# Last stage of a gated two-layer block: projections laid behind the scores in smaller pieces, and two gates ahead of the joining of keys

## The reference

```
x = x + tanh(g_xattn[0]) * L0_xattn(layernorm(x), ctx, ctx)      # causal, 16 heads of 32
x = x + tanh(g_ffn[0])   * L0_ffn(layernorm(x))                  # silu(gate) * up, rms_norm, ternary weights
x = x + tanh(g_xattn[1]) * L1_xattn(layernorm(x), ctx)           # below
x = x + tanh(g_ffn[1])   * L1_ffn(layernorm(x))                  # below

# L1_xattn (the first 257 context rows are the image part: here all 256)
q = rms_norm(x @ q_w.T + q_b) * norm_q_w;  k = rms_norm(ctx @ k_img_w.T + k_img_b) * norm_k_img_w
v = ctx @ v_img_w.T + v_img_b
out = softmax(q k^T / sqrt(32)) v @ o_w.T + o_b

# L1_ffn: h = rms-normed x, quantised to 8 bits a row; ternary weights
value, gate = split(quant(h) @ w_gv.T)                           # 2048 each
u = value * silu(gate);  result = x + quant(u) @ w_out.T
```

## Time and profile before

| | |
|---|---|
| median of 3 runs | 1082.85 us (1082.8 to 1083.58) |
| the profiled execution | 1082.55 us, span of the engines 1080.6 us |
| TensorE busy | 1051.7 us, 97% of the span |
| VectorE / ScalarE / GpSimd busy | 830.9 (77%) / 586.0 (54%) / 119.1 us (11%) |
| mean granted TensorE clock | 0.997 |

### The profile page before, as it was taken

One profiled execution on the slowest core, in us unless ns is written; L12 is line 12 of the kernel. 1 busy time (PEld: TensorE's weight loads), 2 busy tenths in 40 slices (PEclk: granted clock), 3 DMA queues, 4 the chain that ended last, 5 costly groups with the idle time before them and its releaser, 6 DMA issues.

```text
span 1080.6 us, 24592 instructions
## 1 busy us (share of the span) xinstructions
PE 1051.7 (97%) x9898; PEld 624.6 (58%) x9898; DVE 830.9 (77%) x1440; ACT 586.0 (54%) x893; POOL 119.1 (11%) x212
## 2 busy tenths in 40 slices
PE   8799999999999999999999999999999999999998
PEld 3455555555777777777777655444444444444444
DVE  4888888878777675675666586798888888888987
ACT  4676677677433332433333356647575757574633
POOL 1101001010000000000000212230212111110110
PEclk9999999999999999999999999999999999999999
DMA  9565654642331130330311032214343434331123
GB/s 363 203 201 182 196 165 144 192 142 75 120 79 47 42 79 4 76 79 20 79 40 40 20 108 56 54 40 89 79 89 79 89 79 76 89 61 50 38 61 79
DMA packets 121200, 102.79 MB, mean 95 GB/s; under 512 B 94720, under 2 KB 95232, under 8 KB 120832
## 3 DMA queue, kind: packets, MB, share of 16 engines
q1 hardware_dynamic: 121088, 101.21, 34.2%
HBM read 65.54 MB, written 12.58 MB: 72 GB/s over the span
## 4 chain that ended last, share of the span: by engine, by line
PE 87%; DVE 5%; issue 3%; ACT 3%; DMA 1%; SPq 0%; POOL 0%; ACTq 0%; DVEq 0%; POOLq 0%
PE bank L704 10%; PE bank L705 10%; PE bank L810 10%; PE bank L792 10%; PE bank L669 10%; PE bank L919 7%; PE bank L907 4%; PE bank L937 4%; PE bank L888 3%; PE bank L869 2%; PE bank L549 2%; PE bank L634 2%; PE bank L574 2%; PE bank L601 2%; PE bank L622 2%
## 5 line engine op out<-in xcount | busy, mean ns | idle before, releaser
L704 PE MATMUL bank<-ARENA,W 128*128 128x256 f16 x1024 | 227.3, 273 | 0.7 <-issue 0.7
L705 PE MATMUL bank<-ARENA,W 128*128 128x256 f16 x1024 | 227.3, 273 | 0.0
L1104 ACT ACTIVATE ARENA<-ARENA 128x512 f16<-128x512 f32 (+1 forms) x96 | 66.8, 707 | 136.2 <-DVE ARENA L1747 132.7
L919 PE MATMUL bank<-W,ARENA 128*128 128x512 bf16 x512 | 117.8, 379 | 5.9 <-ACT ARENA L1350 5.1
L792 PE MATMUL bank<-W,ARENA 128*128 128x512 bf16 x512 | 120.8, 379 | 0.0
L810 PE MATMUL bank<-ARENA 128*128 128x512 f32 x256 | 118.0, 602 | 0.5 <-ACT ARENA L1104 0.4
L669 PE MATMUL bank<-ARENA 128*128 128x512 f32 x256 | 118.1, 604 | 0.2 <-DMA ARENA<-in_wkv 0.2
L704 PEld LDWEIGHTS bank<-ARENA,W 128*128 128x128 bf16 x1024 | 100.2, 98 | 19.2 <-issue 1.3
L705 PEld LDWEIGHTS bank<-ARENA,W 128*128 128x128 bf16 x1024 | 100.2, 98 | 17.8
L2211 POOL TENSOR_TENSOR ARENA<-ARENA 128x2 f32<-128x2 f32 (+1 forms) x72 | 51.5, 715 | 483.9 <-DVE ARENA L1523 250.2
L1747 DVE SCALAR_TENSOR_TENSOR ARENA<-bank,ARENA 128x512 f32<-128x512 f32 x64 | 48.0, 750 | 66.5 <-PE bank L705 63.1
(11 more groups left out here) (190 smaller groups left out, 1743.1 us busy)
## 6 DMA issues: line engine op xcount, KB each, us to landing
W<-in_w SPq DMA_DIRECT2D x48, 512.0 KB, 4.2
ARENA<-in_w SPq DMA_DIRECT2D x24, 512.0 KB, 3.6
kv_store<-ARENA SPq DMA_DIRECT2D x32, 256.0 KB, 4.3
W<-kv_store SPq DMA_DIRECT2D x15, 512.0 KB, 4.8
ARENA<-in_ctxT SPq DMA_DIRECT2D x8, 512.0 KB, 3.9
X<-in_x SPq DMA_DIRECT2D x8, 512.0 KB, 5.8
ARENA<-in_ctx SPq DMA_DIRECT2D x8, 512.0 KB, 6.1
out<-X SPq DMA_DIRECT2D x15, 256.0 KB, 2.6
```

The costliest lines, as they stand in the source:

```text
L704: pe.matmul(bank[:, i * S:(i + 1) * S], W0[:, at:at + P], xt_half(b, 0)[:, k, :], start=(k == 0), stop=False)
L705: mm = pe.matmul(bank[:, i * S:(i + 1) * S], W0[:, at:at + P], xt_half(b, 1)[:, k, :], start=False, stop=(k == KD - 1))
L919: mm = pe.matmul(to, QQ[d][:, t, k * P:(k + 1) * P], W1[:, at:at + D], start=(k == 0), stop=(k == KD - 1))
L1104: return act.activation(to, src, ACT.Copy)
```

## The change

In turn 1 TensorE's call for the last block of a query projection (with its bias) moves from ahead of the first probabilities to behind them. In turn 2 each of the projections starts a quarter or two later: the blocks are cut so that each group of scores is followed by three or four blocks as before, but the last three blocks of the output projection stand between the first and the second probabilities. VectorE's c_add_out(0, 0) moves from ahead of the reduction of the last scores to behind the copy of the maxima. In turns 3 to 7 ScalarE does the Silus 5 and 6 one step earlier, each ahead of one of the two joins of keys. No instruction is added or taken away.

```diff
@@ tensor_program, turn 1
             c_max_turn(0)
+            c_probs(0, 0)
             c_project_q(1, 1, (3,))
-            c_probs(0, 0)
             c_probs(0, 1)
@@ tensor_program, turn 2
             c_scores(1, 0)
-            c_project_q(2, 0)
+            c_project_q(2, 0, (0, 1, 2))
             c_scores(1, 1)
-            c_project_q(2, 1)
+            c_project_q(2, 0, (3,))
+            c_project_q(2, 1, (0, 1))
             c_scores(1, 2)
-            c_project_out(0, 0)
+            c_project_q(2, 1, (2, 3))
+            c_project_out(0, 0, (0,))
             c_scores(1, 3)
-            c_project_out(0, 1, (0, 1, 2))
+            c_project_out(0, 0, (1, 2, 3))
             c_max_turn(1)
-            c_project_out(0, 1, (3,))
+            c_project_out(0, 1, (0,))
             c_probs(1, 0)
+            c_project_out(0, 1, (1, 2, 3))
             c_probs(1, 1)
@@ scalar_program, turns 3 to 7
                 both(d_round_u, d, 0)
+                d_gate(d, 5)
                 c_join_k(f, 0)
-                d_gate(d, 5)
+                d_gate(d, 6)
                 c_join_k(f, 1)
-                d_gate(d, 6)
                 d_gate(d, 7)
@@ vector_program, turn 2
             c_norm_q(2, 1)
-            c_add_out(0, 0)
             c_scores(1, 3)
             c_max_parts(1)
             c_max_rows(1)
+            c_add_out(0, 0)
             c_add_out(0, 1)
```

## The result

| | before | after |
|---|---|---|
| median (7 runs each, same chip) | 1082.85 us (1082.09 to 1083.58) | 1085.38 us (1084.29 to 1087.31) |
| ratio after / before | | 1.0024, 95% interval 1.0013 to 1.0036 |
| the profiled execution | 1082.55 us, span 1080.6 | 1085.38 us, span 1083.5 |

The forecast was 1079.9 us in a range of 1078.0 to 1082.6. It was wrong in sign: the loss is 0.24%, small but clear of the interval. I cut the last stage of both profiles at the same three instructions: the first scores of turn 2, the second scores of turn 3, and the second scores of turn 4. For before these are 665.18, 710.61 and 767.08. Lines of ScalarE, VectorE and GpSimd are 3 higher after the change (L1333 is L1336, L1881 is L1884); those of TensorE are the same.

What follows compares the result with a forecast made beforehand. TensorE, busy 97% of the span, was taken as the bound, so only its gaps could be won. Terms +1.2 - 1.4 - 2.8 = -3.0 us took 1082.55 to 1079.55; with the median 0.3 higher, 1079.9 us, range 1078.0 to 1082.6.

Steps and rivals of the forecast that it cites:

- Turn 1: Block 3 behind the first probabilities: the square delays the exponentials, second probabilities start 1.17 us later; taken as +1.2 us.
- the low clock: Rival: the clock falls once more, in turn 1 or where TensorE waits at 702.4; at most 1.6 us, 1081.5 us; chance 0.30.
- Turn 2: Projections in pieces behind the scores: 3.10 us wait won, less 1.68 us slip of the output addition; -1.4 us.
- The new order: Turn 2 on TensorE: scores, blocks and bias in sequence put the second query half's bias product at 675.80.
- 3.10 us that I thought to win: Turn 2: VectorE's reciprocal at 693.51 had waited 3.10 us for TensorE, which would now deliver well before.
- 1.68 by which I let the addition slip: Turn 2: the output addition moves from 685.29 to 686.97, 1.68 us later, behind the last output block.
- From there VectorE runs without a pause: From quantised inputs at 694.22, GpSimd's line ending 694.18, to the last multiply; output projection moves from 705.25 to 703.83.
- The 702.4: Start of turn 3: when TensorE could reach the output projection, were it not waiting for VectorE until 703.83.
- bound of 2.6: Turn 2's upper bound: 2.6 us gained if TensorE's own path, without the wait on VectorE, set the end.
- Turns 3 to 7: Two gates ahead of the key joins: product 7, held by VectorE's gating, starts 0.56 us earlier, five times; -2.8 us.
- the 0.06 us of the output projection: Time from a VectorE result to TensorE's start, 0.06 us, also used for product 7 behind the gating.
- Rival 4: The low clock comes again and again, up to 1.6 us per stretch: three give 1084.7 us, four 1086.3; chance 0.08.

Runs made afterwards that it cites:

- e_after_bias: The whole change, plus GpSimd's two bias additions for batch 2 moved ahead of batch 0's line in turn 2: 1083.34 us, ratio 1.0007.
- e_turn1: The kernel before with only turn 1's edit on TensorE, first probabilities ahead of projection block 3 and its bias: 1084.25 us, ratio 1.0015.
- e_gates: The kernel before with only Silus 5 and 6 ahead of the key joins on ScalarE in turns 3 to 7: 1079.49 us, ratio 0.9976.
- e_bias: The kernel before with only GpSimd's bias additions for batch 2 moved ahead of the line of batch 0: 1081.72 us, ratio 0.9994.

## Why the prediction was wrong

**Turn 1: right, with the risk at the wrong price.** Predicted +1.17, alone +1.13. Each link held: probabilities 0.64 earlier, square ahead of the exponentials, gap larger. Of the low clock the prediction said that it had followed the gap once of two times. Behind the 2.00 us gap it came in the profiles of after and of e_after_bias, not in that of e_turn1: +1.57 us where it came. I gave it 0.30 and left it out of the likeliest sum, though the same step that I forecast made the gap longer.

**Turn 2: the step that failed.** Predicted -1.4, measured +1.8. Two terms:
- "The new order": I started the second scores 3 blocks after the first, at 665.18 + 1.08 + 3 x 0.885 without asking for their banks. They wait until VectorE has reduced the first scores (0.96 us). From it comes +1.13 for the maxima's turn (17.50 us behind the first scores instead of 16.37) and +1.10 for the addition of the output (22.89 instead of 21.79). The reciprocal moved by 0.40 and not by 1.42. And 1.64 of the 3.10 us that I thought to win were the low clock of that one execution: in e_gates, with turn 2 in the order of before at full clock, VectorE's reciprocal waits 1.46 (row in the last section), less than the 1.68 by which I let the addition slip: in an execution at full clock the prediction's own terms would have given a loss of 0.2 for this turn.
- "From there VectorE runs without a pause": it does, but I gave L1884 and L1886 their old durations while GpSimd's line ended "just in time". Behind that line stand the two bias additions, which in the profile before began 3.2 us ahead of L1881 and had ended when it came. Bringing VectorE forward brought it beside them: +2.0 us, shown by the two kernels that move the additions.

Together: the reciprocal came 1.0 us later than forecast, and the stretch behind it took 2.2 longer (2.0 for the two operations, the rest the end of GpSimd's line, for which L1884 started 0.16 later behind L1837 than before), 3.2 in all. The wait of 1.15 us ahead of the output projection, which the prediction named as 1.4, is there; it is the end of VectorE's chain, only later. The 702.4 at which TensorE "could be" is worked out nowhere, and does not fit the bound of 2.6, which would be 702.65.

**Turns 3 to 7: right.** Predicted -0.56 a turn, measured -0.55 in turn 3 (e_gates) and -0.47 in 4 to 7; product 7 waits 0.31 for the gating where I worked out 0.4. The 0.09 too much is the step from VectorE's result to TensorE: I took the 0.06 us of the output projection, and here it is about 0.15 (from 791.17 and 0.75 us of gating to 792.07). Alone this part gives 0.9976, 2.6 us. In after turn 3 does not show it: +0.3 instead of -0.55, because of the fetch inside the keys' transposition, a cost of 0.85 us that the prediction had no term for. Why the recut of turn 2 moves that fetch is not shown.

**The sum.** Forecast -3.0, measured +2.9 between the profiles. The difference is turn 2 (3.2), the clock (1.6), the transposition (0.9) and the gates' size (0.5 in turns 4 to 7), less 0.2 ahead of turn 1. Rival 4, the only slower one, was the wrong mechanism: one low stretch came, not three, and the time still rose. The three parts alone multiply to 1.0011 (0.9976, 1.0015, 1.0020), and the whole gave 1.0024: within the parts' intervals, they add up. Two losses hid one gain.

## What to carry to other kernels

Before pulling an engine's chain forward, look at what the other engines do at the new time, not at the old one: GpSimd's long operation on memory that VectorE shares can stretch an operation on 128x2 from 0.15 to 1.2 us. When a block of filler is moved between two steps, check both ends of both: what the filler's own follow-up (here the square) blocks on the next engine, and whether the step that now comes sooner has its banks. And try the parts alone: one of the three held all of the gain. A wait read in one profile can be made by a low stretch of the clock in that execution: 3.10 us here were 1.46 in another.

## What the hardware showed unexpectedly

- A fetch of 16 KB of TensorE's instructions within a transposition by DMA goes with a near stop of the whole transposition for about 1.1 us (319 GB/s in a slice, then 38, 0, 0, 7, 10), which makes it 3.43 to 3.98 us long instead of 2.60 to 2.88 (all 20 profiles). Moving it away with 16 idle waits at the program's start took 1.15 us off turn 3 (57.05 to 55.90). The medians fell by 1.7 (1079.49 to 1077.79, on two chips, each beside its own before: ratios 0.9972 and 0.9956, whose intervals overlap); the part beyond turn 3 is not shown. What in the queue stops is not shown either.
- A VectorE operation that comes beside GpSimd's 128x512 addition does not get slower in proportion, but ends with it: in e_gates, with the order of before and the clock at 1.00, L1881 meets the second addition too. VectorE, then GpSimd:

```profile
691.59 1.76 DVE L1832 RECIPROCAL ARENA<-bank 128x256 f32<-128x256 f32 x1 [1.46 <-PE bank L907]
...
693.73 1.01 DVE L1881 TENSOR_TENSOR ARENA<-ARENA 128x2 f32<-128x2 f32 x1
694.78 0.17 DVE L1883 TENSOR_SCALAR ARENA<-ARENA 128x2 f32<-128x2 f32 x1
```

```profile
692.18 2.54 POOL L2241 TENSOR_TENSOR X<-X,ARENA 128x512 f32<-128x512 f32 x2
```

It ends at 694.74, the addition at 694.72. The reciprocal, which reads a bank, keeps its 1.76 us beside the first addition. So VectorE paid this before the change too in executions whose turn 2 ran at full clock (of its 0.86 us the turn got back only 0.26 when the additions were moved, in e_bias), and it was hidden in the profile that I read, where the low clock had made VectorE late: L1881 began 30.46 us behind the first scores of turn 2 (665.18 to 695.64) instead of 28.82 (664.91 to 693.73).
